# Routed rows that carry their weight, a scatter that adds into one row a token, and GpSimd for the last additions

## The reference

```python
xn = layernorm(x)
scores = sigmoid(xt @ gate_w.T)
top_scores, top_idx = top_k(scores, 2)
top_scores = top_scores / (sum(top_scores) + 1e-20) * 2.5
y_e = (silu(xt @ w1[e]) * (xt @ w3[e])) @ w2[e]      # for every expert e
routed = sum over the two chosen e of top_score_e * y_e
shared = (silu(xt @ sw1) * (xt @ sw3)) @ sw2
out = x + attention(xn) + routed + shared
```

## Time and profile before

| | |
|---|---|
| Median of 3 runs | 766.68 us (765.8 to 767.55) |
| The profiled execution's own time | 764.81 us |
| Its span | 763.0 us |
| PE busy | 713.9 us (94%) |
| DVE busy | 643.5 us (84%) |
| ACT busy | 590.2 us (77%) |
| POOL busy | 512.6 us (67%) |
| DMA | 99.67 MB, 131 GB/s on average |

### The profile page before, as it was taken

How to read it: one execution, slowest core, us unless ns; L and a number is a source line. 1 busy time by engine, 2 the same in 40 slices (tenths; PEclk the granted TensorE clock), 3 DMA queues, 4 the chain that set the end, 5 groups by cost and what they waited for, 6 DMA issues and landing times.

```text
span 763.0 us, 15747 instructions
## 1 busy us (share of the span) xinstructions
PE 713.9 (94%) x4618; PEld 640.8 (84%) x4618; DVE 643.5 (84%) x1743; ACT 590.2 (77%) x1462; POOL 512.6 (67%) x460
## 2 busy tenths in 40 slices
PE   4988888999998999999999999999999999999875
PEld 3877777888887999999999999999999999988774
DVE  6666989888887888898888988889888888888886
ACT  3456776787877888888888888888888888888752
POOL 2443556888887678776777668776777767776620
PEclk9899999999999999999999999999999999999989
DMA  9551313253235244654446444554445544223201
GB/s 293 138 152 53 116 63 102 95 171 124 83 122 176 84 153 122 201 151 132 145 132 201 142 140 128 191 160 135 139 128 198 160 126 147 75 68 114 84 29 55
DMA packets 61396, 99.67 MB, mean 131 GB/s; under 512 B 9840, under 2 KB 33568, under 8 KB 61312
## 3 DMA queue, kind: packets, MB, share of 16 engines
q1 hardware_dynamic: 57904, 89.35, 38.4%
q0 software_dynamic: 3408, 9.33, 3.3%
HBM read 72.14 MB, written 26.51 MB: 129 GB/s over the span
## 4 chain that ended last, share of the span: by engine, by line
PE 62%; POOL 12%; DVE 12%; issue 7%; ACT 6%; DMA 1%; SPq 0%; DVEq 0%; ACTq 0%; POOLq 0%
PE qk_proj L439 12%; PE u_acc L439 11%; PE scores L439 11%; PE ffn L439 9%; PE out_acc L439 9%; PE probs_t L550 6%; POOL swapped L920 5%; POOL xs_sorted L951 3%; POOL rot L928 3%; ACT swapped L766 2%; DVE acc L1240 2%; DVE acc L1298 1%; PE ffn L631 1%; ACT split L758 1%; ACT pt_hi L797 1%
## 5 line engine op out<-in xcount | busy, mean ns | idle before, releaser
L920 POOL TENSOR_TENSOR swapped<-swapped,sin_t 128x512 f32<-128x512 f32 x128 | 165.2, 1290 | 172.1 <-DVE rot L1193 133.3
L935 POOL TENSOR_TENSOR qk_lo<-rot,qk_hi 128x512 fp32r<-128x512 f32 x128 | 163.4, 1294 | 14.9 <-ACT qk_hi L775 14.9
L1217 DVE TENSOR_TENSOR pt_lo<-probs_t,pt_hi 128x512 fp32r<-128x512 f32 x238 | 117.9, 495 | 61.3 <-ACT pt_hi L797 60.6
L786 ACT ACTIVATE probs<-scores,nbias 128x512 f32<-128x512 f32 (+3 forms) x256 | 135.0, 528 | 35.5 <-DVE nbias L1202 31.6
L766 ACT ACTIVATE swapped<-qk_proj 64x512 f32<-64x512 f32 x256 | 151.9, 593 | 6.9 <-PE qk_proj L439 2.4
L797 ACT ACTIVATE pt_hi<-probs_t 128x512 fp32r<-128x512 f32 x238 | 104.8, 441 | 39.3 <-PE probs_t L550 32.3
L1202 DVE CUSTOM_DVE_ANT_0 scores<-scores,mask 128x512 f32<-128x512 f32 (+3 forms) x256 | 125.3, 490 | 8.5 <-PE scores L439 2.9
L550 PE MATMUL probs_t<-ident,probs 128*128 128x128 f32 x604 | 105.5, 274 | 10.2 <-DVE pt_lo L1217 9.0
L1240 DVE SCALAR_TENSOR_TENSOR acc<-out_acc,rsum,acc 128x256 f32<-128x256 f32 x256 | 111.1, 476 | 1.9
L439 PE MATMUL scores<-qk_hi 128*128 128x512 f32 (+3 forms) x256 | 94.8, 370 | 3.8 <-ACT probs L786 3.4
L1186 DVE TENSOR_TENSOR rot<-qk_proj,cos_t 128x512 f32<-128x512 f32 x128 | 87.6, 684 | 12.2 <-ACT swapped L766 12.2
(11 more groups left out here) (179 smaller groups left out, 1863.1 us busy)
## 6 DMA issues: line engine op xcount, KB each, us to landing
wt<-expert_parts SPq DMA_DIRECT2D x39, 704.0 KB, 4.5
wt<-expert_parts SPq DMA_DIRECT2D x39, 512.0 KB
raw_a<-in_attn SPq DMA_DIRECT2D x8, 768.0 KB, 5.8
xs_sorted<-u_lo SPq DMA_DIRECT2D x3, 1670.5 KB, 9.5
xs<-xs_sorted SPq DMA_DIRECT2D x39, 128.5 KB, 2.8
expert_parts<-split SPq DMA_DIRECT2D x8, 352.0 KB, 2.3
expert_parts<-raw_f SPq DMA_DIRECT2D x8, 352.0 KB
acc<-in_x SPq DMA_DIRECT2D x4, 512.0 KB, 7.0
```

Source lines behind the costliest of these rows:

```text
L786: ac.activation(probs[:, m % 2, PR_AT[i]:PR_AT[i] + n], s_bank[i % 2][:, 0:n], ACT.Exp, bias=nbias[:, m % 2, i:i + 1], scale=-1.0, accum_o ...
L920: pool.tensor_tensor(swapped[:, which, :], swapped[:, which, :], sin_t[:, :], ALU.mult).then_inc(sinm_ok[which], 1)
L935: pool.tensor_tensor(qk_lo[:, m % 2, which, :], rot[:, which, :], f32(qk_hi[:, m % 2, which, :]), ALU.subtract).then_inc(rlo_ok[which], 1)
L1217: ve.tensor_tensor(pt_lo[:, c], turn_bank(m, j)[:, 0:n], f32(pt_hi[:, c]), ALU.subtract).then_inc(ptlo_ok, 1)
```

## The change

Each sorted row gets one more number, its weight (`DX` is 258). ACT multiplies the result with it when it copies it from PSUM. Both results of a token go to one row of `ys_tokens`, which is now zeroed beforehand, and the scatter adds instead of writing. The result of a row that holds nothing goes to one of 128 rows ahead of the tokens' rows, its own for each partition. Then one load and one plain addition a group are left at the end. POOL makes these additions, in the order 4, 5, 6, 7, 0, 1, 2, 3 (batches 2 and 3 first).

```diff
-DX = D + 1
+DX = D + 2
-        ys_d = nc.dram_tensor("ys_tokens", (1 + TOP_K * TT * P, D), F32).ap()
+        ys_d = nc.dram_tensor("ys_tokens", (1 + P + TT * P, D), F32).ap()
...
-        BACK = {F_LAST + 3: (0, 1), F_LAST + 4: (2, 3), F_LAST + 5: (4, 5), F_LAST + 6: (6, 7)}
-        EARLY, MIDDLE, END = range(3)
-        ADDS = {(58, EARLY): 0, (59, EARLY): 1, (60, EARLY): 2, (61, EARLY): 3, (61, MIDDLE): 4, (62, EARLY): 5,
-                (62, MIDDLE): 6, (63, MIDDLE): 7}
+        BACK = {F_LAST + 3: (4, 5), F_LAST + 4: (6, 7), F_LAST + 5: (0, 1), F_LAST + 6: (2, 3)}
+        ADDS = {57: (4,), 58: (5,), 59: (6,), 60: (7, 0), 61: (1,), 62: (2,), 63: (3,)}
...
+            def zero_sums():
+                sp.dma_start(ys_d[1:].rearrange("(t p) d -> p t d", p=P),
+                             mask[:, 0:D].unsqueeze(1).to_broadcast([P, 1 + TT, D])).then_inc(st_zsum, 16)
...
-                rows = [ys_d[1 + k * TT * P:][2 * g * P:2 * (g + 1) * P].rearrange("(i p) d -> i p d", p=P)
-                        for k in range(TOP_K)]
-                for i in range(2):
-                    sp.dma_start(xn[:, 2 * g + i, 0:D], rows[0][i]).then_inc(ld_rows[g], 16)
-                    sp.dma_start(back[2 * g + i], rows[1][i]).then_inc(ld_rows[g], 16)
+                sp.dma_start(xn[:, 2 * g:2 * g + 2, 0:D],
+                             ys_d[1 + P:][2 * g * P:2 * (g + 1) * P].rearrange("(i p) d -> p i d",
+                                                                               p=P)).then_inc(ld_rows[g], 16)
...
+                if s == PICK_AT:
+                    zero_sums()
...
-            for b in range(B):
+            for b in (0, 2, 1, 3):
...
-                ac.activation(ysb[:, t % 2, :], f_bank[:, 0:D], ACT.Copy).then_inc(yev_ok, 1)
+                ac.wait_ge(home_ok, t + 1)
+                ac.activation(ysb[:, t % 2, :], f_bank[:, 0:D], ACT.Copy,
+                              scale=share[:, t % 4:t % 4 + 1]).then_inc(yev_ok, 1)
...
-                                        in_=ysb[:, t % 2, :], in_offset=None).then_inc(st_y[t % 2], 16)
+                                        in_=ysb[:, t % 2, :], in_offset=None,
+                                        compute_op=ALU.add).then_inc(st_y[t % 2], 16)
...
-                pool.tensor_copy(home[:, t % 4:t % 4 + 1], xs[:, t % 2, D:DX]).then_inc(home_ok, 1)
+                pool.tensor_copy(share[:, t % 4:t % 4 + 1], xs[:, t % 2, D + 1:DX])
+
+                pool.tensor_scalar(home[:, t % 4:t % 4 + 1], xs[:, t % 2, D:D + 1], first_id[:, 0:1], None,
+                                   ALU.max).then_inc(home_ok, 1)
+
+            def add_routed(group, s):
+
+                pool.wait_ge(ld_rows[group], 16)
+                pool.wait_ge(add_ok, NT * (last_head(group, s) + 1))
+                a = acc[:, 2 * group:2 * group + 2, :]
+                pool.tensor_tensor(a, a, xn[:, 2 * group:2 * group + 2, 0:D], ALU.add).then_inc(yadd_ok, 1)
...
+                for group in ADDS.get(s, ()):
+                    add_routed(group, s)
...
-                need(ve, yadd_ok, steps["back"])
+                if m >= SLOTS - 8 and 2 * b in ADD_ORDER[:4]:
+                    ve.wait_ge(yadd_ok, groups_added(b))
...
                 if s == PLACE_AT:
                     place_counts()
                     place_tiles()
+                    route_weights()
...
                 if s == PLACE_AT + 2:
                     place_owners()
-                    route_weights()
```

More of the change, by code:

```diff
@@ L144, in moe_attention_kernel @@
         best_e = sb("best_e", [P, TT])
-        topw = sb("topw", [P, TOP_K, TT])
+        topw = sb("topw", [P, TT])
         tsum = sb("tsum", [P, 2, TT])
@@ L154, in moe_attention_kernel @@
         home = sb("home", [P, 4], I32)
+        share = sb("share", [P, 4])
         s_bank = [ps(f"scores{i}", [P, T]) for i in range(2)]
@@ L213, in moe_attention_kernel @@
         owner_f = route_m[:, 40 * E:40 * E + 40]
-        back = [raw_f[:, n * D:n * D + D] for n in range(4)] + [raw_a[:, n * D:n * D + D] for n in range(6)] + [
-            wt[:, n // 4, n % 4 * D:n % 4 * D + D].bitcast(F32) for n in range(6)]
         def f32(ap):
@@ L268, in scatter_steps, with last_head, groups_added @@
             return range(n, n + SCATTERS.get(s, 0))
-        BACK = {F_LAST + 3: (0, 1), F_LAST + 4: (2, 3), F_LAST + 5: (4, 5), F_LAST + 6: (6, 7)}
-        EARLY, MIDDLE, END = range(3)
-        ADDS = {(58, EARLY): 0, (59, EARLY): 1, (60, EARLY): 2, (61, EARLY): 3, (61, MIDDLE): 4, (62, EARLY): 5,
-                (62, MIDDLE): 6, (63, MIDDLE): 7}
+        BACK = {F_LAST + 3: (4, 5), F_LAST + 4: (6, 7), F_LAST + 5: (0, 1), F_LAST + 6: (2, 3)}
+        ADDS = {57: (4,), 58: (5,), 59: (6,), 60: (7, 0), 61: (1,), 62: (2,), 63: (3,)}
+        ADD_ORDER = [g for at in sorted(ADDS) for g in ADDS[at]]
+        def last_head(g, s):
+            return max(m for m in range(s - 1) if where(m)[1] == g // 2)
+        def groups_added(b):
+            return 1 + max(ADD_ORDER.index(g) for g in (2 * b, 2 * b + 1))
         def late(m):
@@ L960, in result_home @@
                 pool.wait_ge(yev_ok, t + 1)
+                if t == 0:
+                    pool.wait_ge(st_zsum, 16)
                 need(pool, st_y[(t + 1) % 2], 16 * ((t + 1) // 2))
@@ L995, in _ @@
         def _(ve):
-            steps = {"route": 0, "inv": 0, "adds": 0, "shared": 0, "back": 0}
+            steps = {"route": 0, "inv": 0, "adds": 0, "shared": 0}
             def step(ins):
@@ L1124, in route_weights @@
                 step(ve.reciprocal(tsum[:, 1, :], tsum[:, 0, :]))
-                for k in range(TOP_K):
-                    last = ve.scalar_tensor_tensor(out=topw[:, k, :], in0=best[:, k, :], scalar=0.5 * ROUTED_SCALE,
+                for k, to in enumerate((xn[:, :, D + 1], topw[:, :])):
+                    last = ve.scalar_tensor_tensor(out=to, in0=best[:, k, :], scalar=0.5 * ROUTED_SCALE,
                                                    in1=tsum[:, 1, :], op0=ALU.mult, op1=ALU.mult)
-                step(last)
+                last.then_inc(weights_ok, 1)
             def copy_ranks():
@@ L1286, in add_shared @@
                 steps["shared"] += 1
-            def add_routed(g):
-                ve.wait_ge(ld_rows[g], 16 * PER_GROUP)
-                need(ve, add_ok, steps["adds"])
-                for k in range(TOP_K):
-                    for i in range(2):
-                        t = 2 * g + i
-                        of = xn[:, t, 0:D] if k == 0 else back[t]
-                        if k == 1:
-                            ve.wait_ge(yadd_ok, steps["back"] + i + 1)
-                        ve.scalar_tensor_tensor(out=acc[:, t, :], in0=of, scalar=topw[:, k, t:t + 1], in1=acc[:, t, :],
-                                                op0=ALU.mult, op1=ALU.add).then_inc(yadd_ok, 1)
-                steps["back"] += PER_GROUP
-            def add_group(s, at):
-                if (s, at) in ADDS:
-                    add_routed(ADDS[s, at])
             for s in range(-LEAD, SLOTS + 1):
@@ L1343, in _ @@
                 u_parts(s)
-                add_group(s, MIDDLE)
                 if r == 3:
```

17 lines of the change are left out of this document (7 added, 10 removed).

## The result

| | Median | Runs | Profiled execution |
|---|---|---|---|
| Before | 766.24 us | 764.68 to 767.55 (4) | 764.81 us, span 763.0 us |
| After | 756.64 us | 756.5 to 758.78 (4) | 756.71 us, span 754.9 us |

The ratio is 0.9887 (95% interval 0.9868 to 0.9906). The medians differ by 9.6 us, the profiled executions by 8.1 us; I forecast 6.8 us. Five further runs of the kernel after (experiment 10) have a median of 758.94 us and a ratio of 0.9912; the median of all nine is 758.21 us. Where the 8.1 us lie is read from the starts of `u_lo`, as in the earlier trace rows.

What follows compares the result with a forecast made beforehand. PE alone was taken to set routed slots 15 to 53, DVE slots 58 to 60. Savings of 3.77 + 1.26 + 0.94 + 0.36 + 0.5 = 6.8 us took 766.68 to 759.9 us; range 756.8 to 763.8.

Steps and rivals of the forecast that it cites:

- Slots 58 to 60: DVE loses its additions there, so each slot falls to slot 57's 9.12 us: 3.77 us saved.
- slots 61 and 62: Without DVE's additions, PE's last matmul of `weighted` bounds slot 61 (1.26 us gained); PE's idle 0.94 us goes in slot 62.
- rival A: PE's clock stays up in slots 61 and 62, saving up to 2.8 us more: 757.1 us; chance 0.14.
- DVE to POOL: POOL gains eight additions of 1.30 us each, covered by its idle time in slots 58 to 60: nothing on the path.
- Rival B: POOL's additions hold up `rotate` or its own sine product in slots 58 to 60, losing 3.9 us: 763.8 us; chance 0.10.
- The adding scatter and the small operation: On POOL in routed slots: scatter may grow from 1.03 to 2.8 us, operation adds 0.20; idle 2.04 us covers them: nothing.
- Rival D: The adding scatter takes longer than the 12.6 us available; at 15.2 us, 859 us in all; chance 0.06.
- The zeroing: 2176 KB leave SP in slot 0, taking 12.4 us, ahead of loads ACT needs at 109.01: tight but fits, nothing.
- Rival C: The zeroing delays expert loads by up to 3 us: 762.9 us; chance 0.10.
- rival E: DVE waits in `add_head` for POOL's groups and the waits eat the whole gain: 766.7 us; chance 0.04.
- The weights: Their DVE work, 0.99 us, moves from slot 4 to slot 2, paid in one and saved in the other: nothing.
- Anything before slot 57 longer than now: Sign that the prediction is wrong; no lengthening was forecast ahead of slot 57.

Runs made afterwards that it cites:

- experiment 10: The changed kernel once more, unchanged, run beside the one with slot 13 filled by matmuls on PE: 758.94 us, ratio 0.9912.
- experiment 2: Kernel before, with 6, 4 and 4 matmuls whose result nobody reads added on PE in slots 60, 61 and 62: 764.29 us, ratio 0.9975.
- experiment 4: Changed kernel with POOL's eight additions left out, a one-column memset in place of each: 756.77 us, ratio 0.9871.
- experiment 1: Changed kernel with the eight merged additions kept on DVE, at the places and in the order of the kernel before: 760.42 us, ratio 0.9903.
- experiment 5: Kernel before, with only the sorted rows widened from 257 to 258 numbers, the last zero and unused: 766.96 us, ratio 1.0002.

## Why the prediction was right, and where its sum was off

The time was forecast as 759.9 us; measured were 756.64 us, below the low end of the range by 0.2 us with the first four runs and 758.94 us, inside it, with the five of experiment 10, whose ratio of 0.9912 is that of the forecast. Direction and mechanism held; two sizes did not, and they partly cancel: slots 58 to 63 and the end gave 10.1 us where I had summed 6.8, and 2.0 us were lost ahead of them, where I had put nothing. That the total comes so near is in that part luck.

- **Slots 58 to 60** fell to 9.11 us each, 3.8 us in all, as forecast. The argument was a slot of the same kernel without additions, and the chain ran again as in that slot.
- **The mis-sized term is that of slots 61 and 62:** forecast 1.26 + 0.94 = 2.2 us, measured 5.37. Two causes are shown. First, rival A came true there in part: 1.2 us are PE's clock, which experiment 2 gets without the change. I had it at 0.14 and at up to 2.8 us. Second, the additions themselves were worth 4.15 us, since the three groups in these slots (3, 4 and 5; 4.75 us at 1.58 or 1.59 each) stood mostly on DVE's chain. The step that failed is that I took PE's times in the old profile (the matmul of 738.20, the idle 0.94 us) for the next bound. They were no bound: they were late through the same additions and the same slow clock. The last matmul of `weighted` started 1.36 us earlier in slot 61 after the change (6.55 instead of 7.91 us behind `u_lo`) and 2.74 in slot 62 (5.14 instead of 7.88); with the clock alone (experiment 2) it was 0.90 and 0.32 us. In slot 62 I also missed group 4, which the code puts behind `u_lo` and which so belongs to the next slot's length.
- **Slot 63 and the end:** 0.32 and 0.62 us, forecast 0.36 and 0.5.
- **DVE to POOL:** the additions took 1.18 us instead of 1.30 and cost nothing (experiment 4). Moving them off DVE gave 2.1 us beyond the merging, by the slots of experiment 1; the medians alone would not tell. Rival B is out: they end 0.66 us ahead of `rotate`.
- **The loads at the end** landed in 2.6 to 3.1 us and held nothing up.
- **The adding scatter and the small operation** cost POOL 0.87 us a slot, forecast nothing to 1.8 for the scatter and 0.20 for the operation. The cover of 2.04 us held. Rival D is out: a landing of 4.2 us, 6.7 at most, not 12.6. ACT's copy with a scale, which I called the same copy, takes 0.09 us more; the routed slots' 0.8 us are not from it, since experiment 5 has them without it.
- **The zeroing** landed in 7.7 us, forecast 12.4, and `split` in slot 2 did not wait for a DMA (it stood behind other work of ACT, without idle time ahead). Rival C is out; rival E too.
- **The weights:** slot 2 became 0.84 us longer and slot 4 1.00 shorter, net nothing, as forecast. But PE's wait in slot 2 grew with it, from 1.76 to 2.58 us. Behind it the clock in slot 3 was 0.91 to 0.94 in six of the nine profiles of kernels with the change (14.3 to 14.7 us; 13.6 where it stayed up); in a seventh it was 0.88 already in slot 2, and slot 3 took 13.7 us. Of the three without the change one fell, to 0.94 (experiment 5, 14.4 us). That may be a cost of up to 1.2 us that I had at nothing. No run moves the weights alone, so it stays open.
- **"Anything before slot 57 longer than now"** was my sign for a wrong prediction, and it came: +2.0 us. 0.8 are the longer rows (experiment 5), which I had dismissed by their 0.4% of transfer. Some 2.2 are slots 3 and 14 at a lower clock (0.91 and 0.86). For slot 14 the change is not to blame: the slot is as long in experiments 2 and 5, which lack it, and short in experiment 4, which has it. They are offset by 1.0 us at the start, up to `u_lo` of unit 0, which varied from 80.2 to 82.3 us over all profiles, whatever the kernel.

So the medians' 9.6 us and the profiles' 8.1 don't contradict each other: all executions of the kernel after lie between 756.5 and 760.06 us, those of the kernel before between 764.5 and 770.5. What the profiles show of this scatter is the clock, which falls or not in slots 3, 9 and 14 (and before the change in 61 to 63), by about 1 us each, and the start.

## What to carry to other kernels

When an edit takes work off a chain, don't take the other engines' old times in the same slot as the next bound, since they may be late through that very work: find a slot of the same program without it, as for slots 58 to 60, or walk the chain with every such instruction removed. An idle time of PE, as the 2.18 us in slot 14, can cost twice, once as idle time and once at a lower clock behind it; where no work can be moved in, matmuls into an unused PSUM tile are a cheap test of how much that is. Here an engine with 2 us idle in each slot took the adding scatter, a further small operation and the last additions for nothing; an addition that it made beside a two-input operation of DVE on the chain cost up to 0.35 us a slot.
